# Four product groups of the last quarter summed by accumulating DMAs and one short VectorE sum, in place of GpSimd adds, in a recommender tower kernel

## The chip, the cores and the metric

The kernel runs on one NeuronCore of a Trainium2 chip. The metric is the device time of one execution in microseconds. The engines are TensorE (PE, matmuls; PEld is its weight loads), VectorE (DVE), ScalarE (ACT), GpSimd (POOL) and SyncE (SP, which here only issues DMAs). All data is float32.

## What is computed

For 512 samples, 32 table rows of 64 numbers each are looked up. Every pair of the 32 fields has its own 64x64 matrix, and the pair's feature is a bilinear form. The 496 features and 16 dense ones go through three dense layers.

```
e = stack([tbl_f[ids[:, f]] for f in range(32)], axis=1)      # (512, 32, 64)
idx_i, idx_j = np.triu_indices(32, k=1)                       # 496 pairs
left = einsum('bpd,pde->bpe', e[:, idx_i], W)                 # (512, 496, 64)
z = sum(left * e[:, idx_j], axis=-1)                          # (512, 496)
h = concatenate([z, dense_ctx], axis=1)
h = maximum(h @ W_top1 + b_top1, 0)
h = maximum(h @ W_top2 + b_top2, 0)
y = h @ W_top3                                                # (512, 1)
```

## The kernel before

The batch is cut into four quarters (`part` 0 to 3) of 128 samples. The 496 pairs are packed into 32 groups of 16 pair features; a group's matmul result `left` is 128x1024 numbers in PSUM, and there are three such slots (`LEFT_BUFS = 3`). For each group and quarter, TensorE makes `left`, VectorE multiplies it with the other field's rows out of PSUM into SBUF (the "take" of the group), and the products are then summed over the 64 elements of each pair. How the sum is made is the group's way, one letter in a hand-written order:

- C: the group is computed with features on the partitions; TensorE sums the products with a matmul against `selector` (`reduce`, L702). The products wait in a ring `prod_col` of `COL_BUFS` buffers.
- A: ScalarE sums (L483), one accumulating activation for each of the 16 features.
- D: VectorE sums with one `tensor_reduce` over 1024 elements (L584).
- P: GpSimd sums: `add_halves` (L434 to L449) adds the upper half of the 64 elements to the lower half five times, and a last small add writes the 16 sums.

The sums of A, D and P groups lie with samples on the partitions; at the end of a quarter `fold` (L728) turns them with a matmul against the identity and adds them to those of the C groups.

`ORDER` is that hand-written order, one string per quarter, and every engine walks it in the same sequence (`STEPS`). `12P` is group 12 by way P, `t0-7` a transposing step, `r2` two C reductions by TensorE, `s3.16` the VectorE sum of D group 16, `f2`/`z2` the fold of a quarter and the copy of its result, `a`, `b`, `c` the dense layers 1, 2, 3 for a span of samples, `e3`, `y3`, `d2` the part of the last quarter's fold and first layer that can be done early. VectorE and TensorE execute these words strictly in order; a word's VectorE instruction holds back all later ones. `+` moves a word to the next quarter.

GpSimd also issues the table gathers (`fetch`, L428), after the takes that free their places. SyncE loads the pair matrices and dense weights.

A take needs its ring buffer free (`POOL_BUFS = 2` for P: the second last P group must be summed), and the next TensorE group needs the slot three groups back taken.

The order of the last quarter before the change is:

```
    "26C 1C s2.11 r4 13A 22D 29A 23A f2 25A 21A 11P s3.22 18P z2 b0 t0-7 16D 15P 9A r2 14A 24P 10A 4A a1.3 5P 17C "
    "31C 20P 0C 27A r2 6C 3P 8C 19C 7A r2 30C 12P 2A 28D",
    "c0 r3 s3.16 a1.0 a1.2 a1.1 e3 y3 s3.28 b1 f3 d2 z3 a2.0 a2.1 c1 a2.2 a2.3 b2 c2",
```

Of the kernel before, what the change touches and what calls it, by code (L numbers as in the profile page):

```python
# [7 lines left out]
ALU = mybir.AluOpType  # L8
ACT = mybir.ActivationFunctionType
AXIS = mybir.AxisListType  # L10
# [37 lines left out]
def strided(n, m):  # L48
# [55 lines left out]
]  # L104

# [1 line left out]
def steps():  # L107
    out = []
    for part, line in enumerate(ORDER):
        for word in line.split():  # L110
            at = part + word.count("+")
            kind, rest = word.lstrip("+")[0], word.lstrip("+")[1:]
            if kind == "h":
                ends = [int(n) for n in rest.split("-")]
                out.append(("hot", at, ends[0], ends[-1] - ends[0] + 1))
            elif kind == "t":
                ends = [int(n) for n in rest.split("-")]
                out.append(("turn", at, ends[0], ends[-1] - ends[0] + 1))
            elif kind == "r":
                out.append(("reduce", int(rest)))  # L120
            elif kind == "s":
                out.append(("sum",) + tuple(int(n) for n in rest.split(".")))
            elif kind == "f":
                out.append(("fold", int(rest)))
            elif kind == "z":
                out.append(("z", int(rest)))
            elif kind in "eyd":
                out.append(({"e": "early fold", "y": "early z", "d": "early l1"}[kind], int(rest)))
            elif kind == "a":
                out.append(("l1",) + tuple(int(k) for k in rest.split(".")))  # L130
            elif kind in "bc":
                out.append((f"l{2 + (kind == 'c')}", int(rest)))
            else:
                out.append(("main", at, int(word[:-1]), word[-1]))
    return out
# [36 lines left out]
TURN_OF = {(item[1], item[2] + i): item for item in SEQ if item[0] in ("turn", "hot") for i in range(item[3])}  # L172
MAINS = [item[1:] for item in SEQ if item[0] == "main"]

GOES = {way: [at for at in MAINS if WAY[at] == way] for way in "CADP"}
DVE_SUMS = [step[1:] for step in STEPS if step[0] == "sum"]
COLS_TO = [sum(p <= part for p, _ in GOES["C"]) for part in range(PARTS)]
NACT = [sum(p == part for p, _ in GOES["A"]) for part in range(PARTS)]
ACT_GROUPS = sorted({g for _, g in GOES["A"]}, key=lambda g: -sum(h == g for _, h in GOES["A"]))
# [56 lines left out]
if LATE_COLS:  # L236
    STARTS[LATE_COLS[0]] = LAST + 1

COL_BUFS = 11
ACT_BUFS = 4  # L240
DVE_BUFS = 2
POOL_BUFS = 2
# [25 lines left out]
def build(nc, a):  # L268
    ctx = ExitStack()
    with ctx:  # L270
        def sb(name, shape, dt=F32):
            return ctx.enter_context(nc.sbuf_tensor(name, shape, dt))
# [11 lines left out]
        prod_act = sb("prod_act", [P, ACT_BUFS, 16, D])  # L284
        prod_dve = sb("prod_dve", [P, DVE_BUFS, 16, D])
        sums = sb("sums", [P, 2, NZ * P])
        prod_pool = sb("prod_pool", [P, POOL_BUFS, 16, D])
        z = sb("z", [P, NZ, B])
        w1 = sb("w1", [P, NZ, H1])
# [45 lines left out]
        dve_summed = sem("dve_summed")  # L335
        pool_halved = sem("pool_halved")
        pool_summed = sem("pool_summed")
        sums_zero = sem("sums_zero")
        folded = sem("folded")
        z_done = sem("z_done")  # L340
# [76 lines left out]
        @block.gpsimd  # L417
        def _(pool):
            pool.memset(ident[:], 0.0).then_inc(ident_zero, 1)
            pool.wait_ge(ident_zero, 1)  # L420
            pool.affine_select(out=ident[:], in_=ident[:], compare_op=ALU.not_equal, fill=1.0, base=0,
                               pattern=[[-1, P]], channel_multiplier=1).then_inc(ident_ready, 1)
            pool.iota(row_no[:], pattern=[[1, HOT_PER]], base=0, channel_multiplier=HOT_PER).then_inc(row_no_ready, 1)
            pool.wait_ge(ids_loaded, 16)

            def fetch(part, n, h):
                f = FIELDS[2 * n + h]
                pool.indirect_dma_start(  # L428
                    out=rows[:, part % ROW_BUFS, n, h, :], out_offset=None,
                    in_=a[f"tbl_{f}"],  # L430
                    in_offset=bass.IndirectOffsetOnAxis(ap=ids[:, part, f:f + 1].bitcast(U32), axis=0),
                ).then_inc(rows_loaded[part % ROW_BUFS][n], 16)

            def add_halves(part, g):  # L434
                i = GOES["P"].index((part, g))
                prod = prod_pool[:, i % POOL_BUFS, :, :]
                width = D // 2
                halved = 5 * i
                while width > 1:
                    pool.tensor_tensor(prod[:, :, :width], prod[:, :, :width], prod[:, :, width:2 * width], ALU.add  # L440
                                       ).then_inc(pool_halved, 1)
                    halved += 1
                    pool.wait_ge(pool_halved, halved)
                    width //= 2
                if part >= 2:
                    pool.wait_ge(folded, part - 1)
                last = prod.rearrange("p (h u o) d -> p h u o d", h=2, o=2)
                pool.tensor_tensor(sums_of(part, g), last[:, :, :, :, 0], last[:, :, :, :, 1], ALU.add
                                   ).then_inc(pool_summed, 1)  # L449

            for n in GATHERS[0][:AT_ONCE]:
                for h in range(2):
                    fetch(0, n, h)
            pool.wait_ge(later_ids_loaded, 16)
            pool.wait_ge(sums_zero, 1)
            after = fetches()
            for part, g in MAINS:
                if WAY[part, g] == "P" or (part, g) in after:
                    pool.wait_ge(left_taken, SLOT["main", part, g] + 1)
                if WAY[part, g] == "P":  # L460
                    add_halves(part, g)
                for at in after.get((part, g), []):
                    fetch(*at)
# [27 lines left out]
        def _(dve):  # L491
# [26 lines left out]
            def take_row_group(item):  # L518
                _, part, g = item
                n, m = GROUPS[g][0]  # L520
                way = WAY[part, g]
                ring, bufs, order = {"A": (prod_act, ACT_BUFS, GOES["A"]), "D": (prod_dve, DVE_BUFS, GOES["D"]),
                                     "P": (prod_pool, POOL_BUFS, GOES["P"])}[way]
                i = order.index((part, g))
                if i >= bufs:
                    dve.wait_ge(*summed(*order[i - bufs]))
                out = ring[:, i % bufs, :, :]
                for k in range(m, m + GU):
                    if SLOT[TURN_OF[part, k]] > SLOT[item]:
                        dve.wait_ge(rows_loaded[part % ROW_BUFS][k], 32 * gathers(part, k))  # L530
                other = rows[:, part % ROW_BUFS, m:m + GU, :, :].rearrange("p m h d -> p (m h d)")
                dve.tensor_tensor(out.rearrange("p (h j) d -> p h (j d)", h=2),  # L532
                                  slot(item).rearrange("p (h j) -> p h j", h=2),
                                  other.unsqueeze(1).to_broadcast([P, 2, BANK]), ALU.mult).then_inc(left_taken, 1)
# [42 lines left out]
            def sum_rows(part, g):  # L577
                if DVE_SUMS[0] == (part, g):
                    dve.wait_ge(sums_zero, 1)
                if part >= 2:  # L580
# [3 lines left out]
                dve.tensor_reduce(sums_of(part, g), prod.rearrange("p (h u o) d -> p h u o d", h=2, o=2), AXIS.X, ALU.add  # L584
                                  ).then_inc(dve_summed, 1)

            def take_z(part):
                if part == 0:
                    dve.wait_ge(dense_loaded, 16 * NP)
                dve.wait_ge(folded, part + 1 + (part == LAST))  # L590
                op = dve.tensor_copy(z[:, :2, cols(part)], zsums(0).rearrange("p (c b) -> p c b", b=PB))
                if part < LAST:
                    op = take_z_inside(part)
                op.then_inc(z_done, 1)
# [4 lines left out]

            for step in STEPS:  # L600
                kind = step[0]
                if kind in ("reduce", "fold", "early fold", "early l1"):
                    continue
                if kind == "early z":
                    dve.wait_ge(folded, LAST + 1)
# [1 line left out]
                    continue  # L607
                if kind == "sum":
                    sum_rows(*step[1:])
                    continue  # L610
                if kind == "z":
                    take_z(step[1])
# [23 lines left out]
        def _(pe):  # L636
# [80 lines left out]

            def early_fold():

                pe.wait_ge(dve_summed, sum(step[0] == "sum" for step in STEPS[:EARLY]))  # L720
                pooled = sum(step[0] == "main" and step[3] == "P" for step in STEPS[:EARLY])
                if pooled:
                    pe.wait_ge(pool_summed, pooled)
                fold_chunks(LAST, [k for k in FOLDED[LAST] if k >= 2], False)
# [55 lines left out]
            reduced = 0  # L780
            for step in STEPS:
                kind = step[0]
                if kind in ("sum", "z", "early z"):
                    continue
                if kind == "early fold":
                    early_fold()
# [97 lines left out]
```

## Time and profile before

| | |
|---|---|
| time, median of 2 runs | 206.3 us (206.03 to 206.57) |
| span of the profiled execution | 203.9 us; its own time is one of the two, so 2.1 to 2.7 us lie around the span |
| TensorE | busy 196.6 us (96%), granted clock 0.992 |
| VectorE | busy 183.2 us (90%) |
| ScalarE | busy 172.0 us (84%) |
| GpSimd | busy 143.9 us (71%), of which 114.1 are gathers |
| DMA | 16.54 MB, nearly all in the first 65 us |

The span runs from the first to the last instruction. Busy is the time in which an engine executes something; a busy TensorE is not TensorE at its peak, since its matmuls overlap. All stamps below are microseconds from the span's start.

### The profile page before, as it was taken

To read this page: it belongs to the slowest core of one execution; us is meant where nothing else is said; L and a number is where in the kernel's file an instruction comes from. 1 tells how busy PE (TensorE), PEld (TensorE's weight loads), DVE (VectorE), ACT (ScalarE), POOL (GpSimd) and SP (SyncE) were. 2 spreads that over 40 slices of the span, in tenths; PEclk is the share of its full clock that TensorE was granted. 3 is DMA by queue.
4 is the path that set the end of the run, shared out by engine and by line. 5 is a ranking of instruction groups with operands and counts; after the bars stand their busy time and mean duration, and the time that the engine had idled before them with its cause. 6 is when DMAs were issued, how large, how long until landed. Compare 5 with 4: busy or idle time off the path is not lost.

```text
span 203.9 us, 6825 instructions
## 1 busy us (share of the span) xinstructions
PE 196.6 (96%) x2188; PEld 133.9 (66%) x2188; DVE 183.2 (90%) x193; ACT 172.0 (84%) x1640; POOL 143.9 (71%) x181
## 2 busy tenths in 40 slices
PE   7698999999999999999999999999999999999994
PEld 7696766577765774776756664885754735665993
DVE  4461999999999999999999999999999999999832
ACT  2200799999998999999989999999999999999800
POOL 5777777777777767777677877767767898895300
PEclk9969999999999999999999999999999999999999
DMA  4965687778492111111111101111111100000000
GB/s 137 319 218 150 201 259 210 235 238 259 141 307 57 27 29 27 29 26 31 29 26 29 29 8 26 32 24 29 27 23 26 21 3 2 2 3 3 3 0 0
DMA packets 11099, 16.54 MB, mean 81 GB/s; under 512 B 3752, under 2 KB 3752, under 8 KB 10936
## 3 DMA queue, kind: packets, MB, share of 16 engines
q1 hardware_dynamic: 7224, 12.17, 18.7%
q0 software_dynamic: 3840, 3.94, 9.4%
q8 instruction: 17, 0.28, 0.6%
q14 instruction: 18, 0.15, 0.2%
HBM read 16.10 MB, written 0.00 MB: 79 GB/s over the span
## 4 chain that ended last, share of the span: by engine, by line
PE 91%; DVE 4%; DMA 2%; issue 2%; ACT 0%; POOL 0%; DVEq 0%; POOLq 0%
PE left L678 29%; PE left L688 27%; PE zsum L702 13%; PE left L754 6%; PE left L657 5%; PE left L764 4%; PE left L668 2%; DMA rows<-tbl_dram,ids 2%; PE zsum L728 2%; PE left L640 1%; DVE prod_act L532 1%; PE left L748 1%; PE left L738 1%; PE zsum L643 1%; PE spread_more L643 1%
## 5 line engine op out<-in xcount | busy, mean ns | idle before, releaser
L483 ACT ACTIVATE prod_act<-prod_act 128x64 f32<-128x64 f32 x816 | 167.8, 647 | 15.1 <-DVE prod_act L532 15.1
L483 ACT ACTIVATION_READ_ACCUMULATOR prod_act<-prod_act 128x1 f32 x816 | 166.3, 558 | 0.0
L428 POOL DMA_INDIRECT rows<-tbl_dram,ids x120 | 114.1, 951 | 40.6 <-issue 27.5
L554 DVE TENSOR_TENSOR prod_col<-left,xt 128x1024 f32<-128x1024 f32 x59 | 69.9, 1217 | 0.3
L678 PE MATMUL left<-w,xt 64*128 64x512 f32 x276 | 68.6, 606 | 0.9 <-DVE xt L509 0.8
L688 PEld LDWEIGHTS left<-xt,w 64*128 64x128 f32 x944 | 57.4, 188 | 16.9 <-issue 7.2
L532 DVE TENSOR_TENSOR prod_act<-left,rows 128x1024 f32<-128x1024 f32 x51 | 61.1, 1216 | 1.8 <-PE left L678 1.7
L688 PE MATMUL left<-xt,w 64*128 64x128 f32 x944 | 61.5, 277 | 0.1
L678 PEld LDWEIGHTS left<-w,xt 64*128 64x128 f32 x276 | 23.0, 187 | 19.7 <-issue 8.1
L440 POOL TENSOR_TENSOR prod_pool<-prod_pool 128x512 f32<-128x512 f32 (+4 forms) x45 | 27.3, 607 | 4.9 <-DVE prod_pool L532 2.0
L702 PE MATMUL zsum<-prod_col,selector 128*32 128x256 f32 x472 | 30.6, 384 | 0.1
L702 PEld LDWEIGHTS zsum<-prod_col,selector 128*32 128x32 f32 x472 | 12.8, 109 | 15.5 <-issue 4.5
L754 PE MATMUL left<-z,w 128*128 128x256 f32 (+1 forms) x64 | 11.5, 334 | 0.0
L754 PEld LDWEIGHTS left<-z,w 128*128 128x128 f32 x64 | 9.6, 191 | 2.8 <-DVE prod_pool L532 0.8
L532 DVE TENSOR_TENSOR prod_pool<-left,rows 128x1024 f32<-128x1024 f32 x9 | 10.9, 1214 | 0.0
L584 DVE TENSOR_REDUCE sums<-prod_dve 128x16 f32<-128x1024 f32 x9 | 10.9, 1208 | 0.0
L532 DVE TENSOR_TENSOR prod_dve<-left,rows 128x1024 f32<-128x1024 f32 x9 | 10.8, 1214 | 0.0
L515 DVE COPY xt<-left 128x512 f32<-128x512 f32 (+3 forms) x11 | 9.7, 879 | 0.4 <-PE left L668 0.2
L505 DVE TENSOR_SCALAR prod_col<-prod_act,row_cast 128x1024 f32<-128x1024 f32 x8 | 5.4, 746 | 2.9 <-ACT prod_act L471 2.9
L561 DVE TENSOR_SCALAR h<-left,b 128x128 f32<-128x128 f32 (+1 forms) x12 | 4.5, 390 | 3.6 <-PE left L748 2.9
L764 PE MATMUL left<-h,w 128*128 128x128 f32 (+1 forms) x48 | 7.6, 312 | 0.0
L764 PEld LDWEIGHTS left<-h,w 128*128 128x128 f32 x48 | 6.7, 191 | 1.1 <-DVE prod_act L532 0.8
(47 smaller groups left out, 78.6 us busy)
## 6 DMA issues: line engine op xcount, KB each, us to landing
w<-pair_w_dram SPq DMA_DIRECT2D x32, 256.0 KB, 3.7
rows<-tbl_dram,ids POOLq DMA_INDIRECT x120, 2.5
w<-tbl_dram SPq DMA_DIRECT2D x4, 256.0 KB, 4.4
w<-w_top_dram SPq DMA_DIRECT2D x1, 1024.0 KB
z<-tbl_dram SPq DMA_DIRECT2D x2, 256.0 KB, 2.9
h<-tbl_dram SPq DMA_DIRECT2D x2, 256.0 KB, 5.3
w<-w_top_dram SPq DMA_DIRECT2D x1, 512.0 KB
z<-dense_t_dram SPq DMA_DIRECT2D x16, 2.0 KB
```

The lines of the kernel that those rows point to most:

```text
L428: pool.indirect_dma_start(out=rows[:, part % ROW_BUFS, n, h, :], out_offset=None, in_=a[f"tbl_{f}"], in_offset=bass.IndirectOffsetOnAxis(a ...
L440: pool.tensor_tensor(prod[:, :, :width], prod[:, :, :width], prod[:, :, width:2 * width], ALU.add).then_inc(pool_halved, 1)
L483: op = act.activation(p, p, ACT.Copy, accum_out=act_sums[:, 2 * P * (part % 2) + k:2 * P * (part % 2) + k + 1])
L532: dve.tensor_tensor(out.rearrange("p (h j) d -> p h (j d)", h=2), slot(item).rearrange("p (h j) -> p h j", h=2), other.unsqueeze(1).to_bro ...
L554: op = dve.tensor_tensor(out, inp, other, ALU.mult)
L584: dve.tensor_reduce(sums_of(part, g), prod.rearrange("p (h u o) d -> p h u o d", h=2, o=2), AXIS.X, ALU.add).then_inc(dve_summed, 1)
L657: mm = pe.matmul(slot(item)[D * h:D * h + D, PB * j:PB * j + PB], hot_tables[i][:, k, :], hot[:, i, k, :], start=(j, k) == LOOKUPS[0], sto ...
L678: mm = pe.matmul(slot(item)[:, BANK * half:BANK * half + BANK], xt[own, part % 2, n, :], w[own, g, :, :], start=True, stop=True)
L688: mm = pe.matmul(slot(item)[:, col:col + PB], w[own, g, i, :], xt[own, part % 2, moving_of(unit, half), :], start=True, stop=True)
L702: mm = pe.matmul(zsums(pair)[32 * s:32 * s + 32, :], selector[:, 30 - 2 * q:62 - 2 * q], prod_col[:, c % COL_BUFS, half, odd::2, :], start ...
L754: mm = pe.matmul(slot(item)[:, :n], w1[:, c, P * k:P * k + P], z[:, c, SPANS[i]], start=(c == 0), stop=(c == NZ - 1))
L764: mm = pe.matmul(slot(item)[:, BANK * o:BANK * o + n], w2[:, k, P * o:P * o + P], h1[:, k, :n], start=(k == 0), stop=(k == H1 // P - 1))
```

## The change

Groups 11, 18, 15 and 24 of the last quarter go from way P to a new way M. They form one batch. VectorE's take writes their products to `prod_halved`, in which the 64 elements of each pair are cut into eight eighths and each eighth of all four groups lies together. Three DMAs issued by GpSimd, each adding to its destination, add eighths 4 to 7 to 0 to 3 (`m0.0`), then 2 and 3 to 0 and 1 (`m0.1`), then 1 to 0 (`m0.2`); GpSimd waits for one before it issues the next. At `n0`, between the takes of 19C and 7A, VectorE waits for the third and sums the eight elements left of each pair, with one `tensor_reduce` for each group. For the room, `COL_BUFS` goes from 11 to 9 and the scratch memory of GpSimd's DMA descriptors to 8192 bytes of each partition, from 16384. The order of the takes is unchanged, and so are the other five P groups (18 of quarter 2, and 5, 20, 3, 12).

```diff
-    "26C 1C s2.11 r4 13A 22D 29A 23A f2 25A 21A 11P s3.22 18P z2 b0 t0-7 16D 15P 9A r2 14A 24P 10A 4A a1.3 5P 17C "
-    "31C 20P 0C 27A r2 6C 3P 8C 19C 7A r2 30C 12P 2A 28D",
+    "26C 1C s2.11 r4 13A 22D 29A 23A f2 25A 21A 11M s3.22 18M z2 b0 t0-7 16D 15M 9A r2 14A 24M m0.0 10A 4A a1.3 5P 17C "
+    "m0.1 31C 20P 0C 27A m0.2 r2 6C 3P 8C 19C n0 7A r2 30C 12P 2A 28D",
...
+BATCH = 4
+HALVED_BUFS = 1
+HALVINGS = 3
+BATCHES = [GOES["M"][k:k + BATCH] for k in range(0, len(GOES["M"]), BATCH)]
...
-COL_BUFS = 11
+COL_BUFS = 9
...
+        prod_halved = sb("prod_halved", [P, HALVED_BUFS, 8, BATCH, 16, D // 8])
...
+            def halve(batch, level):
+                buf = prod_halved[:, batch % HALVED_BUFS, :, :, :, :].rearrange("p e g j d -> p e (g j d)")
+                if level == 0:
+                    pool.wait_ge(left_taken, SLOT[("main",) + BATCHES[batch][-1]] + 1)
+                else:
+                    pool.wait_ge(halved[batch % HALVED_BUFS], 16 * (HALVINGS * (batch // HALVED_BUFS) + level))
+                rest = 4 >> level
+                pool.dma_start(buf[:, :rest, :], buf[:, rest:2 * rest, :], accum_op=ALU.add
+                               ).then_inc(halved[batch % HALVED_BUFS], 16)
...
-            for part, g in MAINS:
+            for step in STEPS:
+                if step[0] == "halve":
+                    halve(*step[1:])
+                if step[0] != "main":
+                    continue
+                part, g = step[1:3]
...
+                if way == "M":
+                    dve.tensor_tensor(out.rearrange("p e (h j) d -> p h j e d", h=2),
+                                      slot(item).rearrange("p (h j e d) -> p h j e d", h=2, j=8, e=8),
+                                      other.rearrange("p (j e d) -> p j e d", j=8, e=8).unsqueeze(1).to_broadcast([P, 2, 8, 8, 8]),
+                                      ALU.mult).then_inc(left_taken, 1)
+                    return
...
+            def sum_halved(batch):
+                dve.wait_ge(halved[batch % HALVED_BUFS], 16 * HALVINGS * (batch // HALVED_BUFS + 1))
+                for i, (part, g) in enumerate(BATCHES[batch]):
...
+                    prod = prod_halved[:, batch % HALVED_BUFS, 0, i, :, :]
+                    dve.tensor_reduce(sums_of(part, g), prod.rearrange("p (h u o) d -> p h u o d", h=2, o=2), AXIS.X, ALU.add
+                                      ).then_inc(dve_summed, 1)
...
-                pe.wait_ge(dve_summed, sum(step[0] == "sum" for step in STEPS[:EARLY]))
+                pe.wait_ge(dve_summed, len(sums_by_dve(STEPS[:EARLY])))
...
-    nc = bacc.Bacc("TRN2", target_bir_lowering=False, num_devices=1)
+    nc = bacc.Bacc("TRN2", target_bir_lowering=False, num_devices=1, dynamic_dma_scratch_size=8192)
```

## Rows read from the trace of the kernel before

**Rows 1.** The page: busy time by engine, and the chain's shares by engine.

```profile
PE 196.6 (96%) x2188; PEld 133.9 (66%) x2188; DVE 183.2 (90%) x193; ACT 172.0 (84%) x1640; POOL 143.9 (71%) x181
...
PE 91%; DVE 4%; DMA 2%; issue 2%; ACT 0%; POOL 0%; DVEq 0%; POOLq 0%
```

**Rows 2.** Windows: stretch, then length, busy PE, PEld, DVE, ACT, POOL, clock, DMA, GB/s.

```profile
185.00:190.00 5.00, 5.00 (x61) 2.68 (x58) 5.00 (x6) 5.00 (x55) 2.69 (x4) 1.00 0.01 3
190.00:195.00 5.00, 5.00 (x46) 4.94 (x45) 4.05 (x9) 2.69 (x25) 0.78 (x3) 1.00 0.02 3
```

**Rows 3.** Timeline of VectorE, last quarter: start, length, what.

```profile
168.75 1.22 DVE L532 TENSOR_TENSOR prod_pool<-left,rows 128x1024 f32<-128x1024 f32 x1
...
172.40 1.22 DVE L532 TENSOR_TENSOR prod_pool<-left,rows 128x1024 f32<-128x1024 f32 x1
...
175.79 1.22 DVE L532 TENSOR_TENSOR prod_pool<-left,rows 128x1024 f32<-128x1024 f32 x1
...
181.47 2.35 DVE L554 TENSOR_TENSOR prod_col<-left,xt 128x1024 f32<-128x1024 f32 x2
183.74 1.21 DVE L532 TENSOR_TENSOR prod_act<-left,rows 128x1024 f32<-128x1024 f32 x1
184.88 1.23 DVE L554 TENSOR_TENSOR prod_col<-left,xt 128x1024 f32<-128x1024 f32 x1
```

**Rows 4.** Timeline of GpSimd, last quarter.

```profile
159.00 0.95 POOL L428 DMA_INDIRECT rows<-tbl_dram,ids  x1 [0.30 <-issue]
159.97 3.35 POOL L440 TENSOR_TENSOR prod_pool<-prod_pool 128x512 f32<-128x512 f32 x5
163.40 0.22 POOL L448 TENSOR_TENSOR sums<-prod_pool 128x16 f32<-128x16 f32 x1
...
187.32 3.35 POOL L440 TENSOR_TENSOR prod_pool<-prod_pool 128x512 f32<-128x512 f32 x5 [2.03 <-DVE prod_pool L532]
190.74 0.22 POOL L448 TENSOR_TENSOR sums<-prod_pool 128x16 f32<-128x16 f32 x1
```

**Rows 5.** Groups of VectorE by shape: busy us, mean ns of one, idle before.

```profile
L532 DVE TENSOR_TENSOR prod_pool<-left,rows 128x1024 f32<-128x1024 f32 x9 | 10.9, 1214 | 0.0
L584 DVE TENSOR_REDUCE sums<-prod_dve 128x16 f32<-128x1024 f32 x9 | 10.9, 1208 | 0.0
...
L515 DVE COPY xt<-left 128x1024 f32<-128x1024 f32 x4 | 4.9, 1219 | 0.3 <-PE left L668 0.2
...
L561 DVE TENSOR_SCALAR h<-left,b 128x128 f32<-128x128 f32 x8 | 2.6, 347 | 3.5 <-PE left L748 2.9 <-PE left L754 0.5
```

**Rows 6.** Groups of GpSimd by shape: the gathers.

```profile
L428 POOL DMA_INDIRECT rows<-tbl_dram,ids x120 | 114.1, 951 | 40.6 <-issue 27.5 <-DVE prod_col L554 7.5 <-DVE prod_act L532 2.6
```

**Rows 7.** The page's DMA issues: KB each, median us from issue to landing.

```profile
w<-pair_w_dram SPq DMA_DIRECT2D x32, 256.0 KB, 3.7
rows<-tbl_dram,ids POOLq DMA_INDIRECT x120, 2.5
```

**Rows 8.** Windows while the first layer's weights load (columns as Rows 2).

```profile
58.00:59.00 1.00, 1.00 (x24) 0.74 (x17) 1.00 (x2) 1.00 (x17) 0.69 (x2) 1.00 1.04 393
...
60.00:61.00 1.00, 1.00 (x18) 0.78 (x16) 1.00 (x2) 1.00 (x13) 0.71 (x1) 1.00 1.00 408
```

**Rows 9.** Timeline of TensorE at the end of the last quarter.

```profile
184.67 2.74 PE L678 MATMUL left<-w,xt 64*128 64x512 f32 x12
...
189.00 2.94 PE L754 MATMUL left<-z,w 128*128 128x128 f32 x24
191.78 0.61 PE L728 MATMUL zsum<-ident,sums 128*128 128x128 f32 x4
```

**Rows 10.** Timeline of TensorE near the start.

```profile
9.19 0.44 PE L657 MATMUL left<-prod_col,z 128*64 128x128 f32 x4 [1.64 <-DVE prod_col L505]
```

**Rows 11.** Windows near the start (columns as Rows 2).

```profile
9.00:10.00 1.00, 0.81 (x12) 0.69 (x14) 1.00 (x3) 0.00 (x0) 0.69 (x2) 1.00 0.85 233
...
12.00:13.00 1.00, 1.00 (x12) 1.00 (x10) 1.00 (x3) 0.00 (x0) 0.85 (x1) 0.50 0.93 264
```

More of the change, by code:

```diff
@@ L126, in steps @@
                 out.append(("z", int(rest)))
+            elif kind == "m":
+                out.append(("halve",) + tuple(int(k) for k in rest.split(".")))
+            elif kind == "n":
+                out.append(("sum halved", int(rest)))
             elif kind in "eyd":
@@ L173, with sums_by_dve @@
 MAINS = [item[1:] for item in SEQ if item[0] == "main"]
-GOES = {way: [at for at in MAINS if WAY[at] == way] for way in "CADP"}
-DVE_SUMS = [step[1:] for step in STEPS if step[0] == "sum"]
+GOES = {way: [at for at in MAINS if WAY[at] == way] for way in "CADPM"}
+BATCH = 4
+HALVED_BUFS = 1
+HALVINGS = 3
+BATCHES = [GOES["M"][k:k + BATCH] for k in range(0, len(GOES["M"]), BATCH)]
+def sums_by_dve(steps):
+    out = []
+    for step in steps:
+        if step[0] == "sum":
+            out.append(step[1:])
+        elif step[0] == "sum halved":
+            out += BATCHES[step[1]]
+    return out
+DVE_SUMS = sums_by_dve(STEPS)
 COLS_TO = [sum(p <= part for p, _ in GOES["C"]) for part in range(PARTS)]
@@ L337, in build @@
         pool_summed = sem("pool_summed")
+        halved = [sem(f"halved{i}") for i in range(HALVED_BUFS)]
         sums_zero = sem("sums_zero")
@@ L522, in take_row_group @@
                 ring, bufs, order = {"A": (prod_act, ACT_BUFS, GOES["A"]), "D": (prod_dve, DVE_BUFS, GOES["D"]),
-                                     "P": (prod_pool, POOL_BUFS, GOES["P"])}[way]
+                                     "P": (prod_pool, POOL_BUFS, GOES["P"]), "M": (None, None, GOES["M"])}[way]
                 i = order.index((part, g))
-                if i >= bufs:
-                    dve.wait_ge(*summed(*order[i - bufs]))
-                out = ring[:, i % bufs, :, :]
+                if way == "M":
+                    batch = i // BATCH
+                    out = prod_halved[:, batch % HALVED_BUFS, :, i % BATCH, :, :]
+                    if batch >= HALVED_BUFS:
+                        dve.wait_ge(dve_summed, DVE_SUMS.index(BATCHES[batch - HALVED_BUFS][-1]) + 1)
+                else:
+                    if i >= bufs:
+                        dve.wait_ge(*summed(*order[i - bufs]))
+                    out = ring[:, i % bufs, :, :]
                 for k in range(m, m + GU):
@@ L531, in take_row_group @@
                 other = rows[:, part % ROW_BUFS, m:m + GU, :, :].rearrange("p m h d -> p (m h d)")
+                if way == "M":
+                    dve.tensor_tensor(out.rearrange("p e (h j) d -> p h j e d", h=2),
[3 more added lines that the diff above has]
+                    return
                 dve.tensor_tensor(out.rearrange("p (h j) d -> p h (j d)", h=2),
@@ L585, in sum_rows @@
                                   ).then_inc(dve_summed, 1)
+            def sum_halved(batch):
+                dve.wait_ge(halved[batch % HALVED_BUFS], 16 * HALVINGS * (batch // HALVED_BUFS + 1))
+                for i, (part, g) in enumerate(BATCHES[batch]):
+                    if DVE_SUMS[0] == (part, g):
+                        dve.wait_ge(sums_zero, 1)
+                    if part >= 2:
+                        dve.wait_ge(folded, part - 1)
+                    prod = prod_halved[:, batch % HALVED_BUFS, 0, i, :, :]
+                    dve.tensor_reduce(sums_of(part, g), prod.rearrange("p (h u o) d -> p h u o d", h=2, o=2), AXIS.X, ALU.add
+                                      ).then_inc(dve_summed, 1)
             def take_z(part):
@@ L601, in _ @@
                 kind = step[0]
-                if kind in ("reduce", "fold", "early fold", "early l1"):
+                if kind in ("reduce", "fold", "early fold", "early l1", "halve"):
                     continue
@@ L609, in _ @@
                     sum_rows(*step[1:])
+                    continue
+                if kind == "sum halved":
+                    sum_halved(step[1])
                     continue
@@ L782, in _ @@
                 kind = step[0]
-                if kind in ("sum", "z", "early z"):
+                if kind in ("sum", "sum halved", "halve", "z", "early z"):
                     continue
```

## The prediction

> **What bounds the kernel now.** I read the page first: TensorE is busy for 96% of the span and holds 91% of the chain that ended last, VectorE is busy for 90% of it, and GpSimd has no share of the chain at all [rows 1]. The last quarter by windows shows TensorE, VectorE and ScalarE all full until 190 us and GpSimd with room from 185 on [rows 2]. The VectorE timeline says which of them sets the pace: between the takes of the last quarter it has no idle row, and from the start of one 1.21 us instruction to the next it is 1.13 us (181.47 to 183.74 for two, 183.74 to 184.88 for one) [rows 3]. TensorE works at most three slots ahead of it, and its groups there come as fast as VectorE takes them (12 matmuls for the three groups 12P, 2A, 28D in 2.74 us [rows 9]). So until about 188 us VectorE is the pace and TensorE its near second; behind that TensorE's own chain of layers and folds runs without a gap to the end [rows 9]. GpSimd works off its P groups back to back from 159.97 at 3.65 us each (3.35 for the five adds, 0.22 for the last, and the starts between), catches up only at 185.3, and sums the last one, 12P, from 187.32 to 190.96 [rows 4]. The early fold that needs it is run at 191.78, right behind TensorE's layer matmuls [rows 9]: GpSimd is on time, by 0.8 us, and nobody waits for it.
>
> **What the change removes.** Four times 3.6 us of GpSimd adds, 14.4 us [rows 4]. None of it is on the path: VectorE has no idle row before a P take [rows 5], and 12P was not summed late. In the new order 12P still waits for its own take only, so GpSimd's last sum moves with that take. The removal is worth 0. VectorE's take is no faster beside a resting GpSimd either: the nine P takes average 1214 ns, no other than the reductions and the turned copies at 1208 and 1219 [rows 5], whatever GpSimd does beside them.
>
> **The four takes** keep their place and size (1024 products), but write runs of 8 elements to eight places. No row has such runs. Bounds: a gain is excluded, since 1024 elements in 1.21 us is what every full-size form takes, and as the upper end a doubling, 1.1 us each or 4.5 in all. The nearest row is the turned copy, which writes runs of 64 to scattered places at 1219 ns, no slower than the plain takes [rows 5]; I take 0.
>
> **The smaller rings.** With nine `prod_col` buffers the take of C group c waits for reduction c-9. Counting through the order, TensorE has never more than 6 C groups taken and not reduced ahead of a C group, so reduction c-9 always stands before group c on TensorE and is done when VectorE comes to it: 0. The halved descriptor memory touches the 120 gathers. They start every 1.25 us (0.95 and 0.30 of issue) and land after 2.5 [rows 4, 6, 7], so two or three are under way at once; I take 0, and if it held only one at a time the first quarter would lose about 1.25 us for each of the first 16, some 20 us. I give that 2 in 100.
>
> **The three DMAs.** They add 1024, 512 and 256 KB (4, 2 and 1 eighths of 2 KB, on 128 partitions). No accumulating DMA is in the trace, so its price is bounded. The fixed part: a GpSimd gather of 32 KB lands 2.5 us after its issue [rows 7], of which its bytes are 0.1, so 2.4. The rate: 393 to 408 GB/s is the most that the 16 engines moved [rows 8]. If an addition costs as much as a copy: 2.4 + 2.6 = 5.0, 3.7 and 3.1 us. If, as its definition has it (it must read the source and the old destination), the engines pass twice the bytes: 7.7, 5.0 and 3.7 us. If they also run at half that rate: 12.9, 7.6 and 5.0. I take the middle, since source and destination are both read. Issuing one holds GpSimd for a gather's pitch, 1.25 us [rows 4, 6]; it could be less (0.3) or, for a descriptor for each piece of a row, several.
>
> The Trainium skill has the same count: its page Collectives: The Full Stack, section "The bandwidth ceiling: the fold count and why AG ≠ RS ≠ AR", says that an addition in the DMA engines halves the bus rate because each piece is read from two sources, and that the addition itself costs nothing. By that rule the sum is the middle one; by a rule of free additions alone it would be the first.
>
> **When the third one lands.** The batch is complete with the take of 24, which starts at 168.75 and ends at 169.97 [rows 3]. So m0.0 is issued at 170.0 and lands at 177.7. GpSimd meanwhile sums 5P, whose take ends at 173.6 [rows 3], until 177.2, 3.6 us later. m0.1 is queued behind that sum: issued at 177.7, landed 182.7. Behind m0.1 stands 20P (taken at 177.0 [rows 3]): 178.95 to 182.5. So m0.2, held by 20P and by the second landing, goes at 182.7 and lands at 186.4. Here is the wait that the change adds: VectorE comes to n0 when the take of 19C is over, at 183.7 [rows 3], and is held for 2.7 us. With copy prices the third issue is held by 20P instead: m0.1 at 177.2, 20P until 182.05, m0.2 lands 185.1, wait 1.4. With the slow prices: landings at 182.9, 190.5 and 195.5, wait 11.8. So GpSimd's in-order queue, more than the bytes, makes the fast case late.
>
> **The short sums.** n0 adds four reductions of 128 elements. A 1024-element reduction takes 1208 ns, of which 1067 would be one element per cycle at the pace of these rows, so 128 elements need 0.14 + 0.13 = 0.27; a 128x128 form of another operation takes 347 [rows 5]. From start to start 0.08 less: 0.19 to 0.27 each; I take 0.9 us for the four. They are on VectorE's path in full.
>
> **The sum.** Behind the waiting VectorE stand the takes of 7A, 30C, 12P, 2A, 28D and all of the tail. TensorE has computed 7A, 30C and 12P and then needs 7A's slot: it stands. ScalarE, too, has at most the rest of 27A in hand until 7A is taken. What is gained back is the lead that TensorE lacked before: 28D started at about 186.45 (the last third of the 2.74 us [rows 9]) though 30C had been taken at 186.1 [rows 3], 0.3 us. So 2.7 + 0.9 - 0.3 = 3.3 us, all of it carried to the end, as the chain behind is without a gap. The span becomes 203.9 + 3.3 = 207.2; with the 2.4 us around it that is 209.6, and the same added to the median of 206.3.
>
> **The rivals.**
>
> *The landing is in time* (the other side: not slower). Mechanism: issue is short on GpSimd and small adds land in under 2 us, so that the third has landed when VectorE arrives. It decides at 183.7. With an issue of 0.3 us: m0.1 at 177.2, 20P 177.5 to 181.1, m0.2 lands by 183.7 if it takes at most 2.6. For it: nearly nothing else is on the DMA engines there (3 GB/s [rows 2]), and the gather's 2.5 includes a table read. Against it: 0.95 us of GpSimd for each gather [rows 6], and the 256 KB loads take 3.7 [rows 7]. Then only the sums are left, 0.9 - 0.3 = 0.6: 206.9 us.
>
> *Additions run slow.* The third case above, or as long an issue on GpSimd: wait 11.8 + 0.9 - 0.3 = 12.4, so 218.7; half of the way there is 214. For it: no row shows such a DMA, and a 256 KB load takes 3.7 us [rows 7], 1.3 more than its fixed part where the peak rate asks 0.6. The slow takes of the M groups (up to 4.5, 214.1) go here too. Against it: each partition's piece is one run of 8, 4 or 2 KB.
>
> *The clock falls.* TensorE stands from the end of 12P (185.6, the first of the three groups from 184.67 [rows 9]) to the take of 7A, at 183.7 + 2.7 + 0.9 + 1.2 = 188.5: 2.9 us. In the trace a gap of 1.64 us, from 7.55 to 9.19 [rows 10], is followed by a clock of 1.00 in the window from 9 and 0.50 in the window from 12, that is 1.2 in place of 2.4 GHz, with half the matmuls in a microsecond [rows 11]. The mean clock of 0.992 over 203.9 us leaves 3.3 us at half pace in all. The same behind n0 would do 3.3 us of the tail at half pace, 1.6 us lost: 211.2. Against it: TensorE here comes from 150 us of full work, where near the start it had hardly begun. The page TensorE: Matmul & The Clock Gate of the Trainium skill, section "Part 1: The HAM clock gate (the "warmup" mystery)", has the rule that an idle TensorE falls to 1.2 GHz; by it this case is the result once the wait is long enough.
>
> *The change gives time*, by whatever row I did not see, such as the early fold that in truth waited for GpSimd: at most the 0.8 us between GpSimd's last sum and the fold. More than 2% faster has no row for it.
>
> **How the numbers follow.** Forecast, with the copy prices as its lower end (208.3 to 210.3): 0.42. In time: 0.18. Clock falls: 0.18. Slow additions or takes: 0.17, spread from 211 to 219. Some gain: 0.03, and 0.02 for the gathers. 2% is about what a measurement of this kernel can tell from no change: 202.2 to 210.4. Faster by over 2%: 0.03. Within: 0.18, 0.42 and some of the clock case, 0.59. Slower by over 2%: 0.38. The range from 206.8 to 215.0 leaves out the gain, the gathers and the upper half of the slow case.
>
> **What would show it.** In the changed kernel's trace: three accumulating DMA rows on GpSimd at 170.0, 177 to 178 and 182 to 183, the first two landing in under 8 and 5 us; an idle row of VectorE before the first short reduction, 2.7 us long and released by a DMA; four reductions of 0.2 to 0.3 us; takes of `prod_halved` at 1.21 us; every stamp before 183.7 unchanged, every one behind it late by the same 3.3 us; a granted clock of 1.00 behind the wait. The prediction is wrong if stamps ahead of 170 differ (the smaller rings or another cost of the M takes), if the first landing is later than 180 (the rate), or if VectorE has no idle row at n0.

## The result and the profile after

The changed kernel takes 213.91 us (median of two runs, 212.86 and 214.96) against 206.3: 3.9% slower, ratio 1.0389 with an interval of 1.0239 to 1.0539. A second set of four runs (below) gives 213.03 and 1.0307. One execution of all that follow, the slowest of the kernel with three fills (212.22 us), lies more than 1.5% above the fastest of its kernel and is left out of that kernel's ratio. The profiled execution has a span of 210.9 us against 203.9, 7.0 more, and its mean granted clock is 0.976 against 0.992. I use these 7.0 us as the amount to be explained; the second set has the same difference of medians, 213.03 - 206.05.

The page of the changed kernel shows the new link at once: the chain that ended last now goes through ScalarE, then through the accumulating DMAs (their line has 6%) and VectorE's short sum. Before, 91% of it was TensorE [rows 1].

```profile
PE 48%; ACT 25%; DVE 11%; DMA 7%; issue 5%; POOL 2%; DVEq 0%; POOLq 0%; ACTq 0%
ACT prod_act L523 25%; PE left L754 14%; PE left L744 11%; PE zsum L768 8%; DMA prod_halved<-prod_halved 6%; PE left L723 4%; DVE prod_act L584 4%; DVE prod_halved L579 2%; PE left L830 2%; POOL prod_pool L465 1%; PE left L706 1%; PE left L820 1%; DMA rows<-tbl_dram,ids 1%; PE left L734 1%; DVE prod_col L606 1%
```

The ScalarE share is no new load (172.3 us busy, 172.0 before [rows 1]): TensorE, VectorE and ScalarE are all full up to there, and the chain only runs along another of them.

The timeline of VectorE, beside [rows 3]:

```profile
168.75 1.22 DVE L579 TENSOR_TENSOR prod_halved<-left,rows 128x1024 f32<-128x1024 f32 x1
...
181.48 2.35 DVE L606 TENSOR_TENSOR prod_col<-left,xt 128x1024 f32<-128x1024 f32 x2
188.09 0.87 DVE L647 TENSOR_REDUCE sums<-prod_halved 128x16 f32<-128x128 f32 x4 [4.26 <-DMA prod_halved<-prod_halved]
188.87 1.22 DVE L584 TENSOR_TENSOR prod_act<-left,rows 128x1024 f32<-128x1024 f32 x1
...
193.97 1.23 DVE L584 TENSOR_TENSOR prod_dve<-left,rows 128x1024 f32<-128x1024 f32 x1 [0.48 <-PE left L744]
```

Up to the take of 19C every stamp of VectorE in this quarter is that of before to 0.01 us. Then VectorE stands for 4.26 us until the third DMA lands, sums for 0.78 (188.09 to the next start at 188.87), and takes 7A 5.1 us later than before. That leaves 1.9 of the 7.0 us, and they come behind this place: the take of 28D is already 5.7 us late, held by TensorE.

The timeline of GpSimd, beside [rows 4]:

```profile
170.44 0.98 POOL L488 DMA_DIRECT2D prod_halved<-prod_halved  x1 [10.20 <-DVE prod_halved L579]
173.72 3.33 POOL L465 TENSOR_TENSOR prod_pool<-prod_pool 128x512 f32<-128x512 f32 x5 [2.29 <-DVE prod_pool L584]
177.13 0.22 POOL L473 TENSOR_TENSOR sums<-prod_pool 128x16 f32<-128x16 f32 x1
179.83 0.90 POOL L488 DMA_DIRECT2D prod_halved<-prod_halved  x1 [2.48 <-DMA prod_halved<-prod_halved]
180.45 3.65 POOL L465 TENSOR_TENSOR prod_pool<-prod_pool 128x512 f32<-128x512 f32 x5
184.19 0.22 POOL L473 TENSOR_TENSOR sums<-prod_pool 128x16 f32<-128x16 f32 x1
184.80 0.87 POOL L488 DMA_DIRECT2D prod_halved<-prod_halved  x1 [0.40 <-DMA prod_halved<-prod_halved]
```

The DMA issues with KB and us from issue to landing, beside [rows 7]:

```profile
prod_halved<-prod_halved POOLq DMA_DIRECT2D x1, 1024.0 KB, 9.0
...
prod_halved<-prod_halved POOLq DMA_DIRECT2D x1, 512.0 KB, 4.5
...
prod_halved<-prod_halved POOLq DMA_DIRECT2D x1, 256.0 KB, 3.3
```

Together: 170.44 + 9.0 = 179.4, issue at 179.83, + 4.5 = 184.3, issue at 184.80 (20P's sum ended at 184.41, so both released it within 0.1 us), + 3.3 = 188.1.

Windows of the changed kernel (columns as [rows 2]): the first DMA moves its data, and then what happens to TensorE behind the wait.

```profile
173.00:174.00 1.00, 1.00 (x23) 1.00 (x22) 1.00 (x2) 1.00 (x17) 0.28 (x1) 1.00 1.11 221
...
177.00:178.00 1.00, 1.00 (x19) 0.42 (x17) 1.00 (x2) 1.00 (x17) 0.27 (x2) 1.00 0.13 25
178.00:179.00 1.00, 1.00 (x21) 1.00 (x19) 1.00 (x2) 1.00 (x17) 0.00 (x0) 1.00 0.04 8
...
187.00:188.00 1.00, 0.00 (x0) 0.00 (x0) 0.00 (x0) 0.00 (x0) 0.89 (x2) 1.00 0.66 111
188.00:189.00 1.00, 0.00 (x0) 0.00 (x0) 0.91 (x5) 0.00 (x0) 0.84 (x3) 0.50 0.00 0
...
193.00:194.00 1.00, 1.00 (x12) 0.15 (x12) 0.52 (x2) 0.99 (x11) 0.92 (x2) 0.50 0.00 0
194.00:195.00 1.00, 1.00 (x28) 0.67 (x29) 1.00 (x1) 1.00 (x12) 0.92 (x2) 0.59 0.00 0
```

With a DMA share of 1.11 an addition moves 221 GB/s, where [rows 8] had 393 to 408 with shares of 1.04 and 1.00; for the same share that is about half. And from 187 to 188 TensorE, VectorE and ScalarE all stand at once. From 188 on the granted clock is 0.50, the 1.2 GHz level, and it is back at 194.8 (0.59 is the mean of the last of these windows). The timeline of TensorE, beside [rows 9], shows the price: the two groups 2A and 28D, 1.83 us of the 2.74 for three before, take 3.78.

```profile
184.67 1.03 PE L744 MATMUL left<-w,xt 64*128 64x512 f32 x4
190.14 3.78 PE L744 MATMUL left<-w,xt 64*128 64x512 f32 x8 [4.44 <-DVE prod_act L584]
193.86 0.65 PE L840 MATMUL left<-h,w 128*32 128x64 f32 x16
```

### The profile page after: what moved, and what is told of

Same layout as the page of the kernel before. It is cut to its first block, busy times and chain, and to the rows that moved or that the text cites. A ratio compares the mean times of both kernels' runs of the same rounds, so it can differ in the third digit from the quotient of the medians.

```text
span 210.9 us, 6802 instructions
## 1 busy us (share of the span) xinstructions
PE 199.1 (94%) x2188; PEld 134.5 (64%) x2188; DVE 184.2 (87%) x197; ACT 172.3 (82%) x1640; POOL 134.1 (64%) x160
## 4 chain that ended last, share of the span: by engine, by line
PE 48%; ACT 25%; DVE 11%; DMA 7%; issue 5%; POOL 2%; DVEq 0%; POOLq 0%; ACTq 0%
ACT prod_act L523 25%; PE left L754 14%; PE left L744 11%; PE zsum L768 8%; DMA prod_halved<-prod_halved 6%; PE left L723 4%; DVE prod_act L584 4%; DVE prod_halved L579 2%; PE left L830 2%; POOL prod_pool L465 1%; PE left L706 1%; PE left L820 1%; DMA rows<-tbl_dram,ids 1%; PE left L734 1%; DVE prod_col L606 1%
## 5 line engine op out<-in xcount | busy, mean ns | idle before, releaser
L744 PE MATMUL left<-w,xt 64*128 64x512 f32 x276 | 70.6, 621 | 5.4 <-DVE prod_act L584 4.4
L465 POOL TENSOR_TENSOR prod_pool<-prod_pool 128x512 f32<-128x512 f32 (+4 forms) x25 | 15.8, 630 | 7.0 <-DVE prod_pool L584 5.4
L488 POOL DMA_DIRECT2D prod_halved<-prod_halved x3 | 2.7, 915 | 13.1 <-DVE prod_halved L579 10.2
```

Source lines behind the costliest of these rows:

```text
L744: mm = pe.matmul(slot(item)[:, BANK * half:BANK * half + BANK], xt[own, part % 2, n, :], w[own, g, :, :], start=True, stop=True)
```

## The experiments

Two sets of four kernels; the kernel before ran beside each set on its chip (206.05 and 206.22 us, medians of 13). Theory: 7.0 us = 4.3 of wait for the third DMA + 0.8 of short sums + 1.9 of TensorE at half pace behind the wait. Rivals: the DMAs or the smaller rings cost by themselves; the clock is only a symptom.

**1. The changed kernel again** (no edit).

> The changed kernel again, beside the others on one chip. Theory (a wait of 4.3 us for the third DMA, four short sums of 0.8, and a clock that falls behind the wait for some 1.9): 203.9 + 7.0 of span, ratio 1.034 (213.3). Rival (part of the first result's 7.6 us lies outside of the span or in a disturbed run): ratio under 1.03.

Measured: 213.03 us (212.37 to 214.74), ratio 1.0307 (1.0267 to 1.0347). The difference of 7.0 us holds.

```profile
189.26 0.86 DVE L647 TENSOR_REDUCE sums<-prod_halved 128x16 f32<-128x128 f32 x4 [4.62 <-DMA prod_halved<-prod_halved]
```

VectorE's wait is 4.62 us in this profile, TensorE stands for 4.80 and the clock falls again. The profile is that of the slowest of the four executions, with a span of 212.7 us: 8.8 above that of before, of which 0.8 lie ahead of the wait.

**2. TensorE kept busy in the wait.** Group 12 of the last quarter is computed five times, in its own slot.

```diff
-                for half in range(2):
+                for _ in range(5 if (part, g) == (3, 12) else 1):
+                    for half in range(2):
```

> The changed kernel, with TensorE computing group 12 of the last quarter five times over in place of once, in the same slot and with the same result; it would otherwise stand still there. Theory (the clock falls because TensorE stands for 4.4 us, and the half pace behind it costs 1.9): the wait of VectorE stays at 4.3 us, the granted clock stays 1.00, and the time falls by 1.9 to a ratio of 1.025 (211.4). Rival (the tail is late for another reason, the clock is a symptom): the ratio stays at 1.034.

Measured: 210.77 us, ratio 1.0215 (1.0182 to 1.0248), 2.3 us less than in experiment 1. Its TensorE timeline: the same two groups behind the wait now take 2.26 us in place of 3.78 (the second of them waits for the take of 30C).

```profile
184.58 4.46 PE L745 MATMUL left<-w,xt 64*128 64x512 f32 x20
189.57 2.26 PE L745 MATMUL left<-w,xt 64*128 64x512 f32 x8 [0.53 <-DVE prod_act L584]
```

Its windows have a clock of 1.00 there:

```profile
191.00:192.00 1.00, 1.00 (x16) 0.17 (x17) 1.00 (x2) 1.00 (x13) 0.14 (x1) 1.00 0.00 0
```

VectorE still waits, here for 3.79 us:

```profile
187.52 0.87 DVE L647 TENSOR_REDUCE sums<-prod_halved 128x16 f32<-128x128 f32 x4 [3.79 <-DMA prod_halved<-prod_halved]
```

That is 0.5 us less than in the changed kernel's profile and 0.8 less than in experiment 1's, so the difference of the times is not the clock alone. What lies behind the wait can be compared by itself: from the take of 7A to the end the span has 20.1 us here, 22.0 in the changed kernel, 22.7 in experiment 1 and 20.2 before. More work for TensorE made the kernel faster: the clock is a cause, worth 1.9 to 2.6 us, and not a symptom.

**3. The sum five takes later.** All DMAs and sums stay; only `n0` moves from behind 19C to behind 28D.

```diff
-    "m0.1 31C 20P 0C 27A m0.2 r2 6C 3P 8C 19C n0 7A r2 30C 12P 2A 28D",
+    "m0.1 31C 20P 0C 27A m0.2 r2 6C 3P 8C 19C 7A r2 30C 12P 2A 28D n0",
```

> The changed kernel with n0 moved from behind 19C to behind 28D, five takes later; all DMAs and sums stay. Theory (only the wait costs, and VectorE reaches n0 at 189.4, a microsecond after the third landing at 188.1): no idle row of VectorE before n0, no TensorE gap, clock 1.00, and only the short sums left: before + 0.4 to 0.9, ratio 1.002 to 1.005 (206.7 to 207.2). Rival (the DMAs or the smaller rings cost something by themselves): ratio over 1.01.

Measured: 206.66 us (10 runs), ratio 1.0041 (1.0008 to 1.0074). The VectorE timeline has no idle time before the sums:

```profile
188.85 1.22 DVE L584 TENSOR_TENSOR prod_dve<-left,rows 128x1024 f32<-128x1024 f32 x1
189.98 0.86 DVE L647 TENSOR_REDUCE sums<-prod_halved 128x16 f32<-128x128 f32 x4
190.75 0.22 DVE L627 COPY y<-left 128x64 f32<-128x64 f32 x1
```

One moved word gives back 6.4 of the 7.0 us. The additions, their traffic, the strided takes, both smaller rings and the short sums together cost 0.6 us (0.2 to 1.5 by the interval), about what the four short sums alone do. No run changes one of the rings alone.

**4. Copies in place of additions.** The DMAs overwrite and don't add, so the sums of the four groups take in the last eighth of the products only.

```diff
-                pool.dma_start(buf[:, :rest, :], buf[:, rest:2 * rest, :], accum_op=ALU.add
-                               ).then_inc(halved[batch % HALVED_BUFS], 16)
+                pool.dma_start(buf[:, :rest, :], buf[:, rest:2 * rest, :]).then_inc(halved[batch % HALVED_BUFS], 16)
```

> The changed kernel with the three DMAs as plain copies of the same bytes from the same places (the four groups' products are overwritten and not added, so their sums are those of other elements). Theory of the prediction (an addition passes twice a copy's bytes): data at about 400 GB/s in place of 220, landings after 5.0, 3.7 and 3.1 us in place of 9.0, 4.5 and 3.3. Rival (the last bytes of the first DMA trickle in for 2.5 us whatever it does, on some slow DMA engine): the trickle stays and the first copy lands after 6.5 or more. VectorE's wait would be 2.0 by the one, 3 by the other.

Measured: one run, 207.42 us. The landings, by the DMA issues:

```profile
prod_halved<-prod_halved POOLq DMA_DIRECT2D x1, 1024.0 KB, 4.7
...
prod_halved<-prod_halved POOLq DMA_DIRECT2D x1, 512.0 KB, 3.2
...
prod_halved<-prod_halved POOLq DMA_DIRECT2D x1, 256.0 KB, 2.3
```

and two of its windows, with the first copy's data under way and then at its end:

```profile
173.00:174.00 1.00, 1.00 (x23) 1.00 (x21) 1.00 (x2) 1.00 (x17) 0.00 (x0) 1.00 0.98 377
...
175.00:176.00 1.00, 1.00 (x16) 0.77 (x14) 1.00 (x2) 1.00 (x17) 0.92 (x2) 1.00 0.02 8
```

The packets of these DMAs are in queue q0 of the profile (packets, MB, share of the 16 engines' time). For the first DMA of the changed kernel, between 170 and 179.2 us:

```profile
q0 software_dynamic: 144, 1.05, 56.6%
q8 instruction: 1, 0.02, 1.3%
```

and for the first copy, between 170.5 and 175.6:

```profile
q0 software_dynamic: 144, 1.05, 54.1%
```

So the addition takes 83 us of engine time (56.6% of 16 times 9.2) and the copy 44, for the same bytes: 1.9 times as much. The slow end of the changed kernel's addition, 25 and then 8 GB/s from 177 on with a share of 0.13 and 0.04, is something else: that is the work of one or two engines out of 16, which finish late. It is not in every addition. The first one of experiment 8 (below) has the same 83 us of engine time between 165.5 and 172.8, and no such end:

```profile
q0 software_dynamic: 143, 1.05, 71.2%
...
prod_halved<-prod_halved POOLq DMA_DIRECT2D x1, 1024.0 KB, 7.1
```

Where the first addition landed after 9.0, 8.3 and 8.5 us (changed kernel, experiments 1 and 2), one packet of queue q8, which carries instructions, runs beside it; where it landed after 7.6 and 7.1 (experiments 3 and 8), none does, nor beside the copy. That this packet makes one engine late is likely but not shown, since no run takes it away. The second and third additions landed after 4.5 to 5.6 and 3.3 to 4.0 us. From 512 to 1024 KB a copy needs 1.5 us more, an addition of the same profile 2.4 to 4.5.

The expectation was off on one point: the wait is 0.25 us, not 2.0.

```profile
184.45 0.86 DVE L646 TENSOR_REDUCE sums<-prod_halved 128x16 f32<-128x128 f32 x4 [0.25 <-DMA prod_halved<-prod_halved]
```

With copies the second and third issue are held by the sums of 5P and 20P, as the prediction had it for its fast case (issues at 177.75 and 182.14), but the 256 KB land in 2.3 us and not in 3.1, and the issue holds GpSimd for 0.6 us, not 1.25.

**5 to 7. The kernel before, with VectorE held at the same place.** No DMA, no new take: idle fills between the takes of 19C and 7A (`COL_BUFS` 10 for the room). Two of the kernels differ a little at the start as well: with five fills, the first of TensorE's steps (`spread_ids`) has five matmuls in place of six; with four, two entries of `LOOKUPS` stand twice, so that TensorE looks these up twice. Their takes of 8C start at 181.14 and 181.03 us, that of three fills, without such an edit, at 181.21: less than 0.2 us of it can be seen there.

```diff
+                if item == ("main", 3, 19):
+                    for i in range(5):            # 3 and 4 in the others
+                        if i:
+                            dve.wait_ge(filled, i)
+                        dve.memset(filler[:], float(i)).then_inc(filled, 1)
```

> The kernel before (nothing of the change in it), with five idle fills of a 128x1024 buffer by VectorE between the takes of 19C and 7A, one waiting for the other: some 5.0 us, as long as VectorE is held there in the changed kernel (wait 4.3, sums 0.8). Theory (the cost is that VectorE is held at this place, whatever holds it): TensorE stands for 4.2 to 4.4 us, the clock falls behind it, ratio 1.030 to 1.034. Rival (accumulating DMAs and their traffic in SBUF are needed for part of it): ratio 1.024 or less.

> As before, with three fills, some 3.0 us. It asks whether the wait that the prediction forecast would have kept the clock. If the clock falls only behind a stand as long as that of the changed kernel: clock 1.00, before + 2.7, ratio 1.013. If a stand of 2.3 us is enough: + 4 or more, ratio 1.020.

> With four fills, some 4.0 us, between the two: + 3.7 and a ratio of 1.018 with a clock of 1.00, + 5.5 and 1.027 with a fallen one.

Measured: 213.25 us and 1.0345 (1.0304 to 1.0386) with five, 211.70 and 1.0263 (1.0201 to 1.0325) with four, 210.63 and 1.0182 (1.0119 to 1.0244) with three. A fill takes 1.19 us from start to start and not 1.0:

```profile
183.65 0.91 DVE L640 MEMSET filler<- 128x1024 f32 x1 [0.16 <-issue]
184.84 0.91 DVE L640 MEMSET filler<- 128x1024 f32 x1 [0.28 <-DVE filler L640]
```

So 7A is taken 5.8, 4.6 and 3.5 us late, where the changed kernel's profile has 5.1 and that of experiment 1 has 5.5. Five fills without any DMA cost 7.0 us, as the changed kernel does, but for a somewhat longer hold; between the times with four and with five fills, a hold of 5.1 us would cost 6.1. The intervals cover this difference; up to 0.9 us of something that belongs to the additions is not excluded. The TensorE timeline with five fills is the same picture:

```profile
184.33 1.03 PE L685 MATMUL left<-w,xt 64*128 64x512 f32 x4
190.46 3.78 PE L685 MATMUL left<-w,xt 64*128 64x512 f32 x8 [5.10 <-DVE prod_act L534]
```

Three fills hold VectorE for 3.5 us, nearly what I had forecast (2.7 + 0.9). In the profiled execution TensorE stands for only 2.71 us, and yet its two groups take 3.79 us, at a clock of 0.50 (its timeline, then a window):

```profile
188.14 3.79 PE L685 MATMUL left<-w,xt 64*128 64x512 f32 x8 [2.71 <-DVE prod_act L534]
```

```profile
188.00:189.00 1.00, 0.86 (x2) 0.51 (x4) 1.00 (x2) 0.88 (x9) 0.00 (x0) 0.50 0.00 0
```

The four executions differ: 208.70 us at a mean clock of 1.00 (no fall), 210.26 and 211.00 at 0.992, and 212.22 at 0.984, the profiled one, whose span is 2.7 us above that of the first. Only the first is near + 2.7. The middle two have no profile; their spans are 1.5 and 2.2 us above that of the first (208.4 and 209.1, 206.9), while executions of the kernel before at 0.992 and at 0.998 to 1.00 are 204.0 to 204.4 and 203.4 to 204.7. So they most likely had a shorter fall. At the wait that I forecast the clock held once, fell once for certain, and twice by this argument. With four fills the order is the same: 208.6 and 209.4 us of span at 0.992, 210.1 and 210.8 at 0.984.

In the changed kernel, in its repetition and with three, four and five fills the profile has the mean clock of 180 to 200 us at 0.83; with a stand of 0.5 us or none it has 1.00. Put side by side, from the VectorE timelines (how much later 7A is taken, counted from the take of 8C, than before, and the span from there to its end):

| profile | 7A late by | from 7A to the end | clock behind the wait |
|---|---|---|---|
| before | 0 | 20.2 | 1.00 |
| copies (4) | 1.1 | 20.1 | 1.00 |
| TensorE kept busy (2) | 4.7 | 20.1 | 1.00 |
| three fills (6) | 3.5 | 22.7 | 0.50 |
| four fills (7) | 4.6 | 22.2 | 0.50 |
| changed | 5.1 | 22.0 | 0.50 |
| five fills (5) | 5.8 | 22.2 | 0.50 |
| changed again (1) | 5.5 | 22.7 | 0.50 |

The price of the fall, 1.9 to 2.6 us against the 20.1 of experiments 2 and 4, does not grow with the wait. In all five profiles the clock stays at 0.50 for 6.8 us; what differs is how much of this TensorE still stands for. With three fills it has stood for 2.1 us when the clock falls and resumes 0.6 us later, so that 6.2 us of its work run at half pace; in the changed kernel it has stood for 2.3 us, resumes 2.1 us later, and 4.7 us of work do.

**8. A better order.** Two of the three D groups of the last quarter, 22 and 16, join the batch, which is then complete 4.4 us sooner; 15 and 24 go back to P.

```diff
-    "26C 1C s2.11 r4 13A 22D 29A 23A f2 25A 21A 11M s3.22 18M z2 b0 t0-7 16D 15M 9A r2 14A 24M m0.0 10A 4A a1.3 5P 17C "
-    "m0.1 31C 20P 0C 27A m0.2 r2 6C 3P 8C 19C n0 7A r2 30C 12P 2A 28D",
-    "c0 r3 s3.16 a1.0 ...
+    "26C 1C s2.11 r4 13A 22M 29A 23A f2 25A 21A 11M 18M z2 b0 t0-7 16M m0.0 15P 9A r2 14A 24P 10A 4A m0.1 a1.3 5P 17C "
+    "31C m0.2 20P 0C 27A r2 6C 3P 8C 19C 7A r2 30C 12P 2A 28D",
+    "c0 r3 n0 a1.0 ...
```

> A new order of the last quarter: the batch is 22, 11, 18, 16 (two of them D groups before), complete 4.5 us sooner; 15 and 24 go back to way P; the three DMAs are issued behind 16, behind 4A and behind 31C; n0 stands in the place of the removed s3.16. It takes two reductions of 1.13 us from VectorE and adds 0.8. Theory (VectorE sets the pace up to 188 us, and no wait is left): 1.1 to 1.5 us faster than before, ratio 0.994. Rival (TensorE is as full, and takes over as the pace once VectorE has less): ratio 0.999 to 1.002.

Measured: 205.95 us (10 runs), ratio 0.999 (0.9968 to 1.0011). Its VectorE timeline shows where the 1.5 us that VectorE was spared went:

```profile
162.40 0.88 DVE L620 TENSOR_SCALAR h<-left,b 128x256 f32<-128x256 f32 x2 [0.94 <-PE left L830]
...
189.73 0.85 DVE L647 TENSOR_REDUCE sums<-prod_halved 128x16 f32<-128x128 f32 x4
190.50 0.34 DVE L613 TENSOR_SCALAR h<-left,b 128x128 f32<-128x128 f32 x1
191.27 0.35 DVE L613 TENSOR_SCALAR h<-left,b 128x128 f32<-128x128 f32 x1 [0.43 <-PE left L820]
```

VectorE waits 0.94 us for TensorE's second layer at 162, right after the place of the dropped s3.22, and for TensorE again in the tail. The rival held: TensorE is as full as VectorE (196.6 us busy against 183.2 before [rows 1]), and takes over. No version here beats the kernel before by more than the measurement can tell.

## Why the prediction was right and where it was off

The direction, the place and the mechanism of the wait were right: nothing gained on GpSimd, a wait of VectorE at n0 with the whole tail behind it, and the short sums. The time of 213.9 lies in the range (206.8 to 215.0), but above the forecast of 209.6: the amount was 7.0 to 7.6 us, not 3.3. That it lies in the range is in part luck: the upper end was there for slow additions, with landings that did not come, and it took in the sum of a longer wait and a fallen clock, which no single case of the prediction had (its clock case alone gave 211.2). Step by step:

- *The removed GpSimd adds are worth 0.* Held: VectorE's stamps up to 183.7 are unchanged, and experiment 3, with GpSimd relieved and no wait, is not faster than before.
- *The takes of M groups cost nothing more.* Held: 1215 ns.
- *The smaller rings cost nothing.* Held: unchanged stamps, and 0.6 us for everything in experiment 3.
- *An addition passes twice a copy's bytes.* Held in the engines' time (83 us against 44 for 1024 KB). This agrees with the halving that the Trainium skill's page Collectives: The Full Stack states in its section "The bandwidth ceiling: the fold count and why AG ≠ RS ≠ AR". Mis-sized for the first DMA: 9.0 us against 7.7, because its last bytes come in from 177 to 179.4 on one or two engines; the additions with a shorter end (experiment 3) or none (experiment 8) landed after 7.6 and 7.1. The other two were 4.5 and 3.3 against 5.0 and 3.7.
- *The third landing at 186.4, a wait of 2.7 us.* It was 188.1 and 4.3. The missing 1.7: 0.4 from the later first issue (170.44), 1.3 from the first DMA, 0.4 between its landing and the second issue and 0.5 between the second's and the third, less 0.5 and 0.4 for the two quicker ones. That GpSimd's queue, with 20P between the DMAs, sets the pace was true in the fast case only (experiment 4); with additions it released the third issue within 0.1 us of the landing.
- *The short sums, 0.9.* 0.78.
- *The lead given back, 0.3.* It must show behind the take of 7A, and where the clock stayed up the rest of the span is 0.1 us shorter than before (20.1 against 20.2, experiments 2 and 4): 0.1, not 0.3.
- *The clock stays* (the forecast; the fall was a rival with a chance of 0.18 at 211.2). This step failed. The fall came, with 1.9 us in the changed kernel's profile and 2.6 in its repetition's, measured against experiment 2 from the take of 7A on; the rival had 1.6. (It lasted 6.8 us, from 188.0 to 194.8, and not the 3.3 that I took from the start; but TensorE stood for the first two of them.) What was wrong is its chance: with three fills, which is the wait that I forecast, the profiled execution has it, and most likely three of the four. That TensorE came from 150 us of full work did not keep the clock up. The row of the start, a stand of 1.64 us with a clock of 0.50 behind it [rows 10, 11], was the one to follow. (Half the matmuls in a microsecond, as I read them there, is not in these two windows, which have 12 each; the loss has to be read from the durations.) The rule of the Trainium skill's page TensorE: Matmul & The Clock Gate, section "Part 1: The HAM clock gate (the "warmup" mystery)", that an idle TensorE falls to 1.2 GHz, agrees with these rows and with the five profiles.
- *The chances.* Those of the two cases within 2% (0.18 and 0.42) make 0.60 without any of the clock case, and not the 0.59 that stands for all three.

Of the sum, then: wait 4.4 for 2.7 (+ 1.7; both counted from 183.7, when VectorE would have taken 7A), sums 0.8 for 0.9 (- 0.1), lead 0.1 for 0.3 (+ 0.2), clock 1.9 for 0 (+ 1.9): 7.0 for 3.3.

## What to carry to other kernels

A chain of dependent DMAs is cheap as long as its consumer stands in the order behind the last landing: count the landings (here 9.0 + 4.5 + 3.3 us and 0.9 between them) from the issue, and put the consumer there. Where engines execute in order and all are full, relieving the one that is not on the path gives nothing, and one early wait stops all of them. And a wait that stops TensorE for some 3 us is likely to be charged with the clock on top, 1.9 to 2.6 us here, and not less for the shorter of these waits; if the wait can't be moved, repeating a matmul in it is worth having.

## What the runs showed of the hardware

- An addition by DMA within SBUF took 83 us of the 16 engines' time for 1024 KB, a copy of the same bytes 44. With full engines they moved 221 GB/s (share 1.11) and 377 (share 0.98).
- The additions of 1024, 512 and 256 KB landed 7.1 to 9.0, 4.5 to 5.6 and 3.3 to 4.0 us after their issue, in five profiles; the copies after 4.7, 3.2 and 2.3 in one. The longest of the first had an end of two microseconds at 8 to 25 GB/s, which those of 7.1 us and the copy had not.
- Issuing an accumulating DMA of 128 rows shows 0.87 to 0.98 us on GpSimd, a plain one 0.57 to 0.59; GpSimd's next instruction, where it was not held by a wait, started 0.6 to 0.8 us after either.
- A VectorE take that writes 32-byte runs at eight places took 1215 ns, as the others do.
- A stand of TensorE of 2.71 us behind 150 us of full work was followed by the 1.2 GHz level, one of 0.53 us (experiment 2) was not. The same three fills left the mean clock at 1.00 in another execution. In five profiles the lower level lasted 6.8 us each time, and began 2.1 to 4.1 us after TensorE's last matmul.
